# A four-layer graph network on 1 core: in the outer layers GpSimd waits for free gather buffers once per ten quads instead of four

## The reference, cut to what matters

```
msgs = edge_weight[:, None] * features[edge_src]      # layer 0
x = layernorm(x + segment_sum(msgs, dst))
...                                                   # layer 1: graph attention with a softmax per node
...                                                   # layer 2: two-layer perceptron on source, destination and edge features
nsum = segment_sum(feat[src], dst)                    # layer 3 (the last)
h_neigh = nsum / max(deg, 1)
...                                                   # three projections, gates, layernorm
```

## Time and profile before

| what | value |
|---|---|
| three runs | 5950.32, 5982.4, 5987.69 us; median 5982.4 |
| profiled execution | span 6105.3 us, from the first to the last instruction; the profile gives no other time for this execution |
| busy share of the span | PE 52%, PEld 42%, DVE 41%, ACT 16%, POOL 53% |
| layer 0, gathers issued | 9.6 to 1151 us |
| layer 3, gathers issued | 4838 to 5963 us |

### The profile page before, as it was taken

How to read it: one execution, slowest core, us unless ns; L and a number is a source line. 1 busy time by engine, 2 the same in 40 slices (tenths; PEclk the granted TensorE clock), 3 DMA queues, 4 the chain that set the end, 5 groups by cost and what they waited for, 6 DMA issues and landing times.

```text
span 6105.3 us, 52726 instructions
## 1 busy us (share of the span) xinstructions
PE 3148.5 (52%) x17147; PEld 2593.6 (42%) x17150; DVE 2498.6 (41%) x4988; ACT 968.1 (16%) x2133; POOL 3211.4 (53%) x3332
## 2 busy tenths in 40 slices
PE   3443444436656566565535565565567334433336
PEld 2333333335545455454424555455556323323324
DVE  5554555634433334333533333333334522322228
ACT  0000000122211112111111111111111301111115
POOL 6666666364544444444364544444443366666662
PEclk8555555677777777777757777777778655666557
DMA  3141111134444444444233333333333211111112
GB/s 87 45 134 44 46 46 46 45 94 123 127 117 122 114 124 120 117 122 111 71 95 97 98 100 97 93 101 93 100 98 84 69 47 46 44 46 45 46 45 70
DMA packets 601180, 514.20 MB, mean 84 GB/s; under 512 B 99694, under 2 KB 532781, under 8 KB 600910
## 3 DMA queue, kind: packets, MB, share of 16 engines
q0 software_dynamic: 105248, 216.15, 13.9%
q10 hardware_dynamic: 210704, 154.61, 9.6%
q1 hardware_dynamic: 284958, 140.08, 8.4%
HBM read 410.93 MB, written 91.26 MB: 82 GB/s over the span
## 4 chain that ended last, share of the span: by engine, by line
another core or an unknown queue 37%; PE 24%; DVE 16%; issue 13%; ACT 5%; ACTq 2%; DVEq 1%; POOL 1%; DMA 1%; SPq 0%; POOLq 0%
PE bank L690 22%; DVE acc L1504 4%; DVE work L1542 3%; PE bank L695 2%; DVE bank L1527 2%; DVE quads L1517 1%; ACT acc L1092 1%; DVE quads L1529 1%; DVEq L375 1%; ACTq L1126 1%; ACT quads L1251 1%; ACTq L1121 1%; ACT quads L1219 1%; ACTq L1129 0%
## 5 line engine op out<-in xcount | busy, mean ns | idle before, releaser
L690 PE MATMUL bank<-quads,work 128*128 128x128 f32 x3920 | 656.2, 313 | 919.5 <-issue 589.3
L690 PEld LDWEIGHTS bank<-quads,work 128*128 128x128 f32 x3920 | 599.3, 223 | 1078.1 <-issue 731.7
L1504 DVE TENSOR_TENSOR acc<-bank,acc 128x512 f32 x588 | 403.2, 686 | 1323.2 <-remote 1063.4
L1100 ACT COPY bank<-zeros 128x384 f32<-128x384 f32 x588 | 283.4, 483 | 2104.6 <-DVE acc L1504 1423.0
L582 POOL DMA_INDIRECT g<-xl,srct x392 | 377.2, 962 | 450.4 <-DVE msg L1828 332.4
L582 POOL DMA_INDIRECT g<-a_src,srct x392 | 377.6, 963 | 442.6 <-PE bank L690 324.6
L582 POOL DMA_INDIRECT nodes<-xl,srct x390 | 374.1, 959 | 380.5 <-DVE msg L1828 265.3
L582 POOL DMA_INDIRECT nodes<-a_src,srct x390 | 374.1, 959 | 358.1 <-PE bank L690 232.7
L1913 DVE TENSOR_TENSOR msg<-bank,b_b 128x512 f32<-128x512 f32 x196 | 135.6, 692 | 994.9 <-PE bank L690 557.5
L582 POOL DMA_INDIRECT g<-x,srct x392 | 371.2, 947 | 240.7 <-issue 116.4
L690 PE MATMUL bank<-quads,g 128*128 128x128 f32 x1568 | 351.9, 393 | 282.7 <-issue 182.1
(11 more groups left out here) (377 smaller groups left out, 6082.1 us busy)
## 6 DMA issues: line engine op xcount, KB each, us to landing
partial<-acc ACTq DMA_DIRECT2D x196, 288.0 KB
work<-local_rank ACTq DMA_DIRECT2D x392, 128.0 KB
work<-xr_by_rank SPq DMA_DIRECT2D x784, 64.0 KB
work<-b_by_rank SPq DMA_DIRECT2D x784, 64.0 KB
work<-in_rel_t ACTq DMA_DIRECT2D x196, 128.0 KB
g<-acc SPq DMA_DIRECT2D x126, 64.0 KB, 1.9
g<-in_x,srct POOLq DMA_INDIRECT x392
scan_penalties<-work SPq DMA_DIRECT2D x14, 448.0 KB
```

The source lines that it names most:

```text
L690: return nc.tensor.matmul(to, lhsT, rhs, start=start, stop=stop, skip_group_check=True)
L1100: nc.scalar.copy(partial_bank(l, i)[:, P:QE].rearrange("p (t e) -> p t e", e=P), zeros[:, 0:P].unsqueeze(1).broadcast_to([P, TQ - 1, P])). ...
L1504: v.tensor_tensor(window, partial_bank(l, q)[:, :], window, ALU.add).then_inc(partial_copied, 1)
```

## The change

`GATHER_QUADS` becomes a table by layer, 10 in layers 0 and 3 and 4 as before in layers 1 and 2. 196 is no multiple of ten, so the count that the last wait asks for is cut at the layer's 196 quads.

```diff
-GATHER_QUADS = 4
+GATHER_QUADS = {0: 10, 1: 4, 2: 4, 3: 10}
...
-        assert NQ % GATHER_QUADS == NQ % PE_QUADS == NQ % DVE_QUADS == NQ % SP_QUADS == 0
+        assert NQ % PE_QUADS == NQ % DVE_QUADS == NQ % SP_QUADS == 0
...
                 rows_used, before = ((partial_done, FILLS), (weighted, 2), (expanded[2], WRING), (partial_done, FILLS + 3 * NQ))[l]
+                ahead = GATHER_QUADS[l]
...
-                    if i % GATHER_QUADS == 0 and i + GATHER_QUADS > RING:
-                        pool.wait_ge(rows_used, before + i + GATHER_QUADS - RING)
+                    if i % ahead == 0 and i + ahead > RING:
+                        pool.wait_ge(rows_used, before + min(i + ahead, NQ) - RING)
                         pool.sem_inc(pool_step, 1)
```

## The result

The changed kernel takes 6225.2 us (median of four runs, 6203.9 to 6231.4) against 5977.1 us for the kernel before in the same comparison: a ratio of 1.042 (95% interval 1.039 to 1.046), 248 us slower. The forecast was 6004 us, within 5900 to 6130. It is wrong: the sign is the slower rival's, and its 6236 us is near, though not by its working.

The account below looks back on a forecast made before the run. GpSimd's issue rate plus its stops was taken to bound layers 0 and 3. Layer 0 at +37.6 and layer 3 at -15.9 gave +21.7 us on 5982.4, so 6004 us, range 5900 to 6130.

Parts of the forecast that it names:

- slower rival: Layers 0 and 3: every 50 us run lets only four quads through, +254 us in all, 6236 us; chance 0.20.
- What bounds the kernel: Layers 0 and 3: GpSimd's issue rate, 5.0 us a quad, plus 8.5 and 8.3 us of waiting per ten quads.
- the hold: Layers 0 and 3: while GpSimd issues unbroken, its customers work 15 to 20 us, then hardly at all until it stops.
- The start of layer 0: First wait wants six quads, not two: quad 10 starts at 98.2 us, with ten quads issued instead of twelve.
- Steady state, layer 0: Stops of 9.6 us per ten quads against 8.5 before, over 18 tens: +20 us, ends -61 and +58 us around it.
- I take six per 50 us: Layer 0: five quads come through in the first 16 us of issue and one more in the hold.
- Four are left for the stop: Layer 0: four of each ten quads come during GpSimd's stop, priced as four missing at 9.6 us.
- one more missing quad: Layer 0: each further quad missing at a stop costs the normal 3.19 us, so 12.8 us after four missing at 9.56.
- Steady state, layer 3: Stops of 7.0 us per ten quads, three or perhaps four quads missing; ends 3.6 us (-61 us) and 8.5 us (+27 us).
- The faster rival: Layers 0 and 3: GpSimd's waiting instruction causes the hold, so fewer waits give -147 us, 5835 us; chance 0.12.
- No hold outside the profiled execution: Layers 0 and 3 run at 5.0 us a quad, the change only moves the start: +22.7 us, 6005 us; chance 0.12.

Follow-up runs that it names:

- part 1: Kernel before run again, unchanged, without the hold: 4493.5 us; beside it ten quads in layer 0 alone 4516.2, in layer 3 alone 4494.1, changed kernel with short stop midway 4596.5.
- part 4: Changed kernel with groups of four for the first twenty quads of layer 0: 4496.9 us, ratio 1.0004 to the kernel before.
- part 9: Kernel before with ten quads in layer 0 alone: 6158.4 us, ratio 1.034; the same with sixteen GpSimd memsets and drains midway in each ten: 6008.3 us, ratio 1.007.
- part 6: TensorE made to wait in layer 0 until a run's last gather landed: in the kernel before 6049.5 us, ratio 1.011; in the changed kernel 6274.9 us, ratio 1.048.
- part 5: Forty SyncE copies of single words nobody reads, beside layer 0: in the kernel before 4492.7 us, ratio 1.000; in the changed kernel 4511.1 us, ratio 1.004.
- part 8: Kernel before with ten quads in layer 0 alone and a short GpSimd stop midway in each ten: 6308.4 us, ratio 1.024.

## Why the prediction was wrong, point by point

*What bounds the kernel.* Right: GpSimd's issue and its stops bound the outer layers, customers fall behind in the hold, and bandwidth isn't why. That machines without the hold run the same kernel in 4493 us is what this reading asks for, since the stops then vanish, in all four layers. But the outer layers are the smaller part of what the hold costs. Between the profile of before and that of part 1 layer 0 differs by 201 us, layer 3 by 151, and layers 1 and 2, which the change leaves alone, by 1271 (3644.5 us against 2373.6). Two details of the reading were wrong. The add at 545.11 is not the one behind the matmul at 528.84: counted through the layer it takes the sum that ended at 518.13, 27.0 us before, so the hold is longer than it says. And it put the hold on waits alone and passed over TensorE's idle time without a wait, which stands in the earlier trace rows.

*The start of layer 0.* Right. Quad 10 was to start near 98 us after a stop of some 37; it started at 94.4 after 34.1. The term was 22.7 us, with ten quads issued instead of twelve; by the two profiles it is 94.4 - 85.5 + 10 = 19 us. The runs without the hold show the same size (+22.7, +22.4 and +24.1 us; +18 with the many small transfers in both kernels), and it goes when the first waits are put back (part 4). There it comes about in another way, though: the kernel before doesn't stop at quad 12 at all, and the changed one stops once, for 20.9 us.

*Steady state, layer 0.* This is the step that failed: +20 us were forecast, with stops of 9.6 us. The 18 stops averaged 18.5 us, the term measured 333.4 - 152.2 = +181 us, and layer 0's loss 195 us. Three things were off, and at the stop of 19.1 us above each is worth some 3 us. "I take six per 50 us" should have been five: four come within 12.4 us after a stop and one in the hold. "Four are left for the stop" was then priced as four missing, but the rows that gave the prices count the sums that the wait asks for less those added when the stop begins, and by that count one more is missing than adds fall into the stop (at quad 92 three were missing, and two adds came; the earlier trace rows). By it six were missing in 15 of the 18 stops (at quad 100: 90 added, 96 asked for), and six cost 9.6 + 2 x 3.19 = 15.9 us by the forecast's own prices. The last 3.1 us are the lead. The earlier trace rows are stops in which the first add came 1.0 and 2.8 us after the last gather; in a stop that begins deep in the hold it comes after 5.9. My bounds ended at 12.8 us. The price of "one more missing quad" was right; the count and the base were not.

*What each stop brings.* The count that would have led there is in the same profile: in layer 0 four or five adds come free beside the gathers after nearly every opening, however long the run is. Groups of four quads open the hold more often than groups of ten: of the 36 waits in the earlier trace rows 30 are stops of over 2 us, against 18. I had priced a stop by what it lacks and never counted what each stop brings. As an estimate, twelve openings fewer, of four adds each at 3.19 us, are 153 of the 181 us. The run of part 9 shows it from the other side: 19 more openings, each 8.2 us long, are paid back in full by shorter stops, and 150 us on top.

*Steady state, layer 3.* -16 us were forecast, with stops of 7.0 us; they were 190.7 / 19 = 10.0 us in the mean. In nine of them three quads were missing, as forecast, and these took 6.6 to 7.7 us, near the forecast; in nine more, four to six were missing, and these took 125.3 us together, the longest 20.9; the last took 0.3. So it is the number that come through in 50 us that was too high on the average. The gathers ran 1164.9 us where they had run 1124.7, and the last add came 30.1 us after the last gather's start where it had come after 15.9. +54 us. The timed runs divide the same way only by subtraction across machines, 248 - 196 = 52 us; layer 3 alone was never run with the hold, but the two profiles of part 6 differ in it by 63 us.

*The slower rival.* Its time, 6236 us, was near by luck. It takes four quads through in 50 us, where five came in layer 0, and makes the forecast's miscount; the two cancel, so that it arrives at the six missing quads that were there. Its stop of 16.0 us is then too short by the 3.1 us of longer lead, and it split the loss evenly over the layers, where it is 195 to 54. Its deciding point, fewer than five quads through in 50 us, wasn't reached in layer 0.

*The faster rival,* that GpSimd's waiting instruction makes the hold, falls: a ten of 40 gathers has no wait in it and has the longest hold, and in part 9 sums came through while GpSimd worked and while it issued again.

*No hold outside the profiled execution.* As a forecast of this comparison it is wrong, since four timed runs of each kernel have the 248 us, not one profile alone. But its number, +22.7 us, is the change where there is no hold. The Trainium skill's rule on the block that writes the records ("NOTIFIC — the notification-queue block", section "7.1 Overflow: three behaviours, one of which stalls the engine") would have the recording slow its engines. Recording by itself doesn't make the hold: the profile of the kernel before in part 1 has the same 52726 instructions as the one in the earlier trace rows and none of the hold. The records do differ in one kind, however. The trace behind the earlier trace rows holds 38,697 semaphore updates, that of part 1 103,814, and all others go the same way: the seven traces with the hold have 36,790 to 39,101, the thirteen without it 103,781 to 104,445. So where the hold is, two thirds of these records are missing. Whether what loses them also holds the engines up, or the hold loses them, no run here shows, and a run in which nothing is recorded isn't on record either: each timed run comes with a span and a granted clock. That rival stands.

*Open.* Why some machines have the hold, and whether it is there when nothing is recorded. The parts only say what it isn't: not brought by DMA traffic alone (part 5), not of the kernel, not a fixed trait of a chip by its number (part 6). Nor is it known why adds go on for some 12 us after gathers resume; that time is read from the rows, not explained.

## What to carry to other kernels

When a bottleneck engine's work keeps its customers from moving, don't price a longer run by the work that is missing at its end: take the lead before the first customer moves, and count what is served for free each time the run is broken. Count "missing" the same way in the balance and in the price. Fewer waits were no saving here, since each stop was an opening worth four sums. Before a cost that hangs on such an effect is acted on, time the kernel on a second machine: here the same edit is worth 22 us on one and 248 on another.

## What the runs showed of the hardware

- One kernel, 4493 us or 5962 to 6168 us, by the machine it came to, with a spread of at most 1% within each. In these experiments the hold showed on three chips, and two of their numbers also came without it.
- With the hold an add starts up to 42 us after the sum that it takes has ended (40.4 us at 705.78; the median in part 1's layer 0 is 0.13 us). TensorE too stands for 1.0 to 2.5 us between matmuls without a wait, 55 times in layer 0 of the changed kernel, never in part 1.
- The hold opens when GpSimd issues no indirect gather for a while. 2.4 us (part 8) let a single add through; stops of 3.4 to 3.8 us (kernel before) open it. The first add comes about 3 us after the last gather behind runs of 20 us, 5.2 to 6.9 us behind runs of 50 us, and in layer 0 adds then mostly go on for about 12 us after gathers begin again. Single adds also come inside the hold, like the one at 749.
- A trace with the hold has 36,790 to 39,101 semaphore updates, one without it 103,781 to 104,445, with the same number of instructions for the same kernel.
- GpSimd's first drain behind a gather took 3.4 us (from 713.23 to 716.62 in part 9), and VectorE's first add began 0.02 us after it ended. That is a coincidence of this break: the drain took 3.4 us in nearly all of the 19 breaks, and the add came 0.3 to 6.8 us after the last gather.
